# Second lookup of a graph kernel: marks of one edge ten places apart instead of eight

## The reference

```python
msg = relu(x[src] + edge_attr)                 # 400000 x 32
agg = segment_sum(msg, dst, 12500)             # 12500 x 32
h   = (1 + eps) * x + agg
out = layernorm(x + h @ W.T + b)               # over the 32 features
```

## Time and profile before

| | us |
|---|---|
| median of 3 runs | 2123.81 (2123.1 to 2124.71) |
| the profiled execution, its own time | 2124.86 |
| its span, first to last instruction | 2122.6 |
| PE busy | 2038.1 (96%) |
| PE weight loads busy | 1945.0 (92%) |
| DVE busy | 1644.8 (77%) |
| ACT busy | 1569.3 (74%) |
| POOL busy | 1540.8 (73%) |

### The profile page before, as it was taken

How to read it: one execution, slowest core, us unless ns; L and a number is a source line. 1 busy time by engine, 2 the same in 40 slices (tenths; PEclk the granted TensorE clock), 3 DMA queues, 4 the chain that set the end, 5 groups by cost and what they waited for, 6 DMA issues and landing times. The chain is left out here.

```text
span 2122.6 us, 117116 instructions
## 1 busy us (share of the span) xinstructions
PE 2038.1 (96%) x46449; PEld 1945.0 (92%) x46449; DVE 1644.8 (77%) x4231; ACT 1569.3 (74%) x1616; POOL 1540.8 (73%) x1571
## 2 busy tenths in 40 slices
PE   1799999999999999999999999999999999999996
PEld 1699999999999999999999999999999999999993
DVE  4777787877778887778877778787777887787774
ACT  3677777777777777777777777777777777777773
POOL 4377777777777777777777777777777777777770
PEclk9999999999999999999999999999999999999998
DMA  3454554545554444554455544544554555454541
GB/s 103 95 110 113 110 113 109 107 107 114 111 115 108 107 108 114 111 115 108 107 107 114 113 112 108 107 109 112 112 115 107 107 109 113 112 112 108 107 108 32
DMA packets 236032, 228.68 MB, mean 108 GB/s; under 512 B 103967, under 2 KB 185305, under 8 KB 235811
## 3 DMA queue, kind: packets, MB, share of 16 engines
q1 hardware_dynamic: 182795, 200.99, 32.1%
q0 software_dynamic: 50080, 25.74, 16.1%
q10 hardware_dynamic: 3130, 1.60, 0.3%
HBM read 225.43 MB, written 2.71 MB: 107 GB/s over the span
## 5 line engine op out<-in xcount | busy, mean ns | idle before, releaser
L517 POOL DMA_INDIRECT rows_all<-in_x,index x1565 | 1540.3, 984 | 527.9 <-issue 473.7
L1154 PE MATMUL found<-table,oh 128*128 128x128 bf16 x18720 | 1264.2, 226 | 10.4 <-DVE oh L747 1.5
L1154 PEld LDWEIGHTS found<-table,oh 128*128 128x128 bf16 x18720 | 1191.3, 146 | 42.5 <-issue 16.8
L989 ACT ACTIVATE oh<-keys,minus_lanes 128x1024 bf16<-128x1024 f16 x195 | 224.0, 1149 | 324.1 <-PE found L1154 324.1
L1134 PE MATMUL l<-xparts,oh 128*57 128x96 bf16 x18720 | 436.5, 207 | 0.8 <-ACT oh L977 0.8
L1134 PEld LDWEIGHTS l<-xparts,oh 128*57 128x57 bf16 x18720 | 409.7, 108 | 14.0 <-issue 1.0
L970 ACT ACTIVATE oh<-slots,minus_lanes 128x1824 bf16<-128x1824 f16 x195 | 351.3, 1802 | 0.0
L762 DVE COPY_PREDICATED rows_all<-mask,found 128x256 f32<-128x256 uint16 x780 | 342.5, 439 | 7.6 <-issue 1.4
L945 ACT CAST table<-l 128x768 bf16<-128x768 f32 x390 | 311.2, 798 | 37.4 <-PE l L1134 16.0
L977 ACT ACTIVATE oh<-oh 128x1824 bf16<-128x1824 bf16 x195 | 335.2, 1719 | 0.0
L756 DVE TENSOR_TENSOR mask<-iota,side 128x32 f16<-128x32 f16 x195 | 37.5, 193 | 331.7 <-PE found L1154 331.7
(11 more groups left out here) (126 smaller groups left out, 907.4 us busy)
## 6 DMA issues: line engine op xcount, KB each, us to landing
slots<-slot_dram SPq DMA_DIRECT2D x195, 456.0 KB
msg<-in_edge SPq DMA_DIRECT2D x390, 128.0 KB
keys<-key_dram SPq DMA_DIRECT2D x195, 256.0 KB
rows_all<-in_x,index POOLq DMA_INDIRECT x1565
index<-in_src SPq DMA_DIRECT2D x195, 4.0 KB
key_dram<-key SPq DMA_DIRECT2D x195, 2.0 KB
slot_dram<-slot_row SPq DMA_DIRECT2D x195, 3.6 KB
dst_rows<-in_x ACTq DMA_DIRECT2D x1, 1562.5 KB
```

Source lines behind the costliest of these rows:

```text
L517: pool.indirect_dma_start(to, None, x, bass.IndirectOffsetOnAxis(indices[:, j:j + 1], 0)).then_inc(done, 16)
L989: nc.scalar.activation(oh2[:, b, :], keys[:, four, :], ACT.Square, bias=minus_lanes[:, b:b + 1]).then_inc(keys_squared, 1)
L1154: last = nc.tensor.matmul(found[:, t * FOUND:(t + 1) * FOUND], marks[:, t, :], table[:, b, n * FOUND:(n + 1) * FOUND],  start=(b == 0 and ...
```

## The change

Each edge's eight marks in `oh2` are followed by two unused places: a row of `oh2` has 1280 elements for each block instead of 1024. DVE and ACT write (and ACT reads) 128 runs of eight; PE reads the 128 marks of a tile at a step of ten elements, 20 bytes, instead of 16. `keys`, which DVE and ACT read, stays packed. Number, order and size of all instructions stay, and so do all waits. `src_rows`, which borrows `oh2` during the setup, is cut to the size that it had. `oh2` grows by 2 KiB in each partition.

```diff
+    PITCH = LOOK + 2
-        oh2 = sb("oh2", [P, KEYS, COLS], BF16)
+        oh2 = sb("oh2", [P, KEYS, P * PITCH], BF16)
-        src_rows = oh2[:, :, :].rearrange("p b c -> p (b c)").bitcast(I32).rearrange("p (h c) -> p h c", h=2)
+        src_rows = oh2[:, :, :].rearrange("p b c -> p (b c)").bitcast(I32)[:, 0:2 * COLS].rearrange("p (h c) -> p h c", h=2)
+        def key_marks(b):
+            return oh2[:, b, :].rearrange("p (e t) -> p e t", t=PITCH)[:, :, 0:LOOK]
+
+        def by_edge(values):
+            return values.rearrange("p (e t) -> p e t", t=LOOK)
...
-                    nc.vector.tensor_scalar(oh2[:, b, :], keys[:, four, :], lanes[:, b:b + 1], None, ALU.is_equal).then_inc(oh2_ready, 1)
+                    nc.vector.tensor_scalar(key_marks(b), by_edge(keys[:, four, :]), lanes[:, b:b + 1], None, ALU.is_equal).then_inc(oh2_ready, 1)
...
-                    nc.scalar.activation(oh2[:, b, :], keys[:, four, :], ACT.Square, bias=minus_lanes[:, b:b + 1]).then_inc(keys_squared, 1)
+                    nc.scalar.activation(key_marks(b), by_edge(keys[:, four, :]), ACT.Square, bias=minus_lanes[:, b:b + 1]).then_inc(keys_squared, 1)
...
-                    at = oh2[:, DVE_KEYS:KEYS, :]
+                    at = key_marks(DVE_KEYS)
                     nc.scalar.activation(at, at, ACT.Relu, scale=-2.0, bias=1.0).then_inc(oh2_act_ready, 1)
...
-                    marks = oh2[:, b, :].rearrange("p (e t) -> p t e", t=LOOK)
...
-                                found[:, t * FOUND:(t + 1) * FOUND], marks[:, t, :],
+                                found[:, t * FOUND:(t + 1) * FOUND], key_marks(b)[:, :, t],
```

More of the change, by code:

```diff
@@ L77, in gnn_kernel @@
     assert EDGES == FIRST + BATCH * ROWS and SHORT > 0 and PAD % CLEARS == 0 and ROUNDS > 0
-    assert 0 < REST % EVEN and REST < P * 2 and D == EVEN and EARLY_KEYS < DVE_KEYS
+    assert 0 < REST % EVEN and REST < P * 2 and D == EVEN and EARLY_KEYS < DVE_KEYS == KEYS - 1
     assert NODES == NP * NT * NEAR and NEAR * D == P and NT > OGROUP + 1 and P < ROWS <= 2 * P and (LOOK + 1) // 2 <= KEYS
```

## The result

The changed kernel takes 2106.57 us (2103.65 to 2108.27, four runs) beside 2124.26 for the kernel before in the same series (2123.1 to 2125.11, four runs): 17.7 us less, a ratio of 0.9916, interval 0.9898 to 0.9933. The forecast was 2124.0. The profiled execution took 2103.65, its span is 2101.4. It is the quickest of the four: the traces are 21.2 us apart in span (2122.6 and 2101.4), the medians 17.7.

The account below looks back on a forecast made before the run. PE was taken as the bound, by the loads of L1154. Loads, bursts, marks and gathers each counted 0 on the path, so the sum was 0: 2124 us, by itself 2119.5 to 2128, with rivals 2057 to 2185.

Parts of the forecast that it names:

- failed step: PE's loads of L1154, second lookup: at 20 bytes they stay at 143 ns, a change of 0 us.
- The bounds (98 and 171): L1154's load in ns: packed 98 would save PE 125 us, the slowest, 171, would cost 524 us more.
- the loads that get a little faster: Rival on L1154: 1 to 3 ns of pace or smooth bursts, 18 to 37 us off, 2096 in the middle; chance 0.12.
- warning sign: The prediction's condition for being wrong: L1154's load depends on where its elements lie, not only on whether they touch.
- bursts' state: PE's second-lookup bursts: share of smooth and rough unchanged, 0; all smooth 18 us less, all rough 21 more.
- What bounds the kernel: PE, busy 96% of the span, sets the time through L1154's load and matmul, paid 18720 times; other engines wait.
- DVE's marks: 585 DVE instructions writing runs of eight: 493 to 550 ns each, some 560 by the skill's rule, hidden under the mask's wait.
- rival at 2218: DVE's marks leave the quick rate, 1221 ns each: 426 us more, 332 covered by the mask's wait; chance 0.09.
- ACT's marks: Two a step on ACT, covered by the square's 1.7 us wait: nothing, 0.3 us less to 0.3 more, hidden.
- POOL: POOL issues the same gathers and isn't late: last starts at 2068.41, the addition needing it at 2083.93; no change.
- first rival: L1154's loads get much faster, PE wants 125 us less, POOL's gathers come next: 2078, from 2050 to 2109; chance 0.24.
- slower-loads rival: L1154's 20-byte loads disturbed more: 3 ns more is 56 us, 2180; all rough 2145; bound 2650; chance 0.22.

Follow-up runs that it names:

- write20_read16: Changed kernel, marks still written at 20 bytes an edge but PE reading at 16; 3051.99 us, ratio 1.0004 to the kernel before (3050.41 in that series).
- pitch11: Changed kernel with three unused places behind each edge's eight marks, so PE reads at 22 bytes; 2112.67 us, ratio 0.994 to the kernel before.
- packed_pe: Kernel before with keys turned by a PE matmul, copied by ACT and written tile by tile, so PE reads packed marks; 2130.32 us, ratio 1.0025.
- grown: Changed kernel with marks written and read at 16 bytes again, only oh2 kept wide; 3050.53 us, ratio 0.9995 to the kernel before.

## Why the prediction was wrong, point by point

**The failed step** is that of PE's loads: "Between them I take the row it is nearest to, L1154's own 143: both steps leave every weight in a place of its own, far from its neighbour, and only the packed rows are known to be quicker. That is 0." The load goes by the step itself. At 20 bytes it measured 144 at the mean (146 before), 142 at the median (143) and 134 at its quickest (140), and this was worth 1.16 ns a matmul, 21.0 us in the trace, in place of 0; `write16_read20` shows that the reads alone do it. The bounds (98 and 171) held for the median. The case that came true was the loads that get a little faster, "1 to 3 ns of pace ... 18 to 37 us off", at its near edge (17.7 in the medians), to which I gave 0.12. No row of the trace had two wide steps of one type to compare. The 139 ns of L1080 was the quickest of 25 loads of 4-byte values with a median of 183, set beside a median of 143, and could carry no rule; the range from 98 to 143 was taken as two classes where it is a slope. The warning sign was in the text: the forecast is wrong "if the load depends on where its elements lie and not only on whether they touch".

**The bursts' state** was kept "as it is, 0". The floor of 60 ns went, and the three bursts shortened by 0.07, 0.01 and 0.07 us in the step shown.

**What bounds the kernel** was right. PE's pace of this line sets the time, one ns of it is 18.7 us, and what it gained came out in full (22.3 us of busy time, 21.2 of span).

**DVE's marks** were right: 496 at the mean in 493 to 550, no loss of the quick rate (rival at 2218, no), and the some 560 ns for runs off an 8-byte boundary did not come either. At 18 and 22 bytes the medians are 553 and 584, over that range. **ACT's marks** at nothing were right; ACT's square still waits 1.6 us each time.

**POOL** at nothing was right for the time only by luck. PE's 21 us are more than the 14.6 that POOL was early by; they came out because POOL's gathers happened to get 19.9 us shorter, which the prediction had only in its first rival. With gathers as long as before the changed kernel would have ended some 9 us later, an estimate: 21 less the 13.8 us of smallest lead before, of which `pitch11` leaves 1.4.

**The slower-loads rival** (2145 to 2180) did not come true for 20 bytes but is real for a neighbour: 18 bytes measured 2134.08, 9 us over the 2124.98 of its series, where I had put 21 to 56.

**The first rival** was right in its mechanism and wrong in its price. The loads at 98 leave PE at 2025 us with a gather left out (I had 2000, without what `packed_pe` adds on PE), and POOL comes next; but "what POOL itself can regain, 0 to 63", of which I took half, was nothing or less in the two kernels that POOL bounds, 1.303 and 1.292 us a gather, and 20 us in the changed kernel, where PE did not need all of it. The term goes with the phase and can't be halved. So it gives 2130 in `packed_pe` instead of 2078. A good part of that kernel's excess over `pitch11` (20 us of span) may be what it adds on PE and ACT; but both lie far above the times that PE alone would allow.

The Trainium skill, "SBUF — State Buffer", section "Door 1: The DMA port swizzle", has each access that crosses to a new line of 16 bytes pay. From 4 bytes up to a step of 16 the table agrees: the number of lines that a load touches rises from 32 at 4 bytes (98 ns) to 128 at 16 (143); from 16 lines at 2 bytes to 32 at 4 it costs nothing. Past 16 bytes each weight has its own line, the rule gives one value, and the trace has 138 at 22 bytes and 163 at 48. The Trainium skill, "TensorE: Matmul & The Clock Gate", section "Weight-path perf modes", has the weights read in four chunks of 32 columns, packed or strided, and names no price for the stride; from 8 bytes on the trace shows one.

**What stays open** is what of the step decides past 16 bytes: why there is a dip at 22 and a peak at 48. Tried and fallen are the touched lines, the distance of the chunks, odd multiples of 4 bytes, and a dip at 20 alone. Open too is why 22 bytes are 0.9 ns quicker and 18 bytes 0.6 dearer in pace with the marks than with values of `xparts`, and what lengthens a gather.

## What to carry to other kernels

Where a matmul of 128 columns loads new weights each time, look at the step at which the weights are read: up to 14 bytes the load is covered, at 16 it sets the pace, and past that a few bytes of padding change the pace either way (61.0 at 16 bytes, 57.2 at 22, 61.7 at 18; 69.5 at 48). Read the mean of the load, not only its median. Judge such a gain by what the next engine has left: the lead of the last gather bounds it, unless that engine's own work gets quicker too. Here 21 us came through with 12.5 us of lead still left, because the gathers went from 1.29 to 1.278 us, which nobody had planned, and 49 more on PE brought nothing. A second kernel that relieves the next engine (one gather left out) shows in one run whether a gain is absent or only withheld.

## What the runs showed of the hardware

- At a mean granted clock of 0.99, the load of 128 bf16 weights takes, at the median, 98, 98, 114, 117, 125, 132 and 143 ns at steps of 2, 4, 8, 10, 12, 14 and 16 bytes; beyond, 138 at 22 and 163 at 48 are the ends.
- A load of up to 132 ns is covered by matmuls of 128 columns at 55.8 ns each; at a median of 137 or 138 the pace is 57 to 58, at 143 it is 60.5 to 61, at 163 69.5. Past 16 bytes it goes with the mean load, half a ns for each ns.
- DVE's 128 runs of eight bf16 values take 482 ns at a step of 20 bytes (478 packed), 553 at 18 and 584 at 22, where every second run starts at an odd element.
- An indirect gather of POOL takes 0.94 us, and 1.21 to 1.25 where one mark of DVE follows another 0.3 to 0.4 us after its start (945 of 947 cases in eight traces; seen, not isolated).
- 1024 pieces of 2 bytes a step, 175,000 packets more, took a kernel of 3050 us to 4760. PE's idle time "issue" before the matmuls of the two lookups went from 543 us in `grown` to 1477, and the granted clock from 0.96 to 0.77; how the two share the rest was not taken apart.
